# Offsets of rows and weights in SBUF, and the order of the three products of a float32 matrix product

## The reference

```
x = x + conv(x, W0) + cond @ cw0.T + bias
x = x + agg_w1 @ x + agg_b1        # agg_w = sum_k att[b, k] * weight[k]
x = x + agg_w2 @ x + agg_b2
x = x + conv(x, W1) + cond @ cw1.T + bias
```

## Time and profile before

| | us |
|---|---|
| median of 3 runs | 2548.53 (2548.13 to 2550.66) |
| the profiled execution | 2548.97 |
| its span | 2547.1 |
| TensorE (PE) busy | 2520.7 (99%) |
| ScalarE (ACT) busy | 2252.2 (88%) |
| VectorE (DVE) busy | 1995.5 (78%) |
| mean busy share of DMA, main queue | 87.3% |

### The profile page before, as it was taken

How to read it: one execution, slowest core, us unless ns; L and a number is a source line. 1 busy time by engine, 2 the same in 40 slices (tenths; PEclk the granted TensorE clock), 3 DMA queues, 4 the chain that set the end, 5 groups by cost and what they waited for, 6 DMA issues and landing times.

```text
span 2547.1 us, 43755 instructions
## 1 busy us (share of the span) xinstructions
PE 2520.7 (99%) x11068; PEld 2062.1 (81%) x11068; DVE 1995.5 (78%) x5032; ACT 2252.2 (88%) x2449; POOL 16.0 (1%) x27
## 2 busy tenths in 40 slices
PE   7999999999999999999999999999999999999997
PEld 6888888888888888888888888888888888888886
DVE  8777787778777878787877778777877787888784
ACT  6889998999899989998998899899989998998895
POOL 2000000000000000000000000000000000000000
PEclk9999999999999999999999999999999999999999
DMA  7889889888888888899889888988888888888986
GB/s 257 318 332 331 328 324 334 329 328 325 332 328 327 329 333 326 325 333 328 329 326 333 330 329 324 333 329 329 325 333 329 327 327 333 325 326 333 329 312 235
DMA packets 334986, 825.56 MB, mean 324 GB/s; under 512 B 37370, under 2 KB 39426, under 8 KB 302210
## 3 DMA queue, kind: packets, MB, share of 16 engines
q1 hardware_dynamic: 332736, 823.94, 87.3%
q10 hardware_dynamic: 2242, 1.53, 0.2%
HBM read 137.97 MB, written 134.23 MB: 107 GB/s over the span
## 4 chain that ended last, share of the span: by engine, by line
PE 97%; DVE 1%; DMA 1%; ACT 1%; SPq 0%; issue 0%; ACTq 0%; DVEq 0%
PE pair L930 82%; PE quad L980 14%; PE pair L970 1%; DVE partial L754 0%; DMA x_ch<-x_ph 0%; DMA mix<-att_saved 0%; ACT x_ch L473 0%; ACT x_out L525 0%; DVE operands L790 0%; DMA x_ph<-in_small 0%; DVE operands L787 0%; DMA x_ph<-x_ch 0%; SPq L318 0%; SPq L370 0%; DVE operands L714 0%
## 5 line engine op out<-in xcount | busy, mean ns | idle before, releaser
L930 PE MATMUL pair<-operands 128*128 128x512 f32 x9216 | 2157.3, 393 | 3.4 <-DVE operands L805 1.8
L930 PEld LDWEIGHTS pair<-operands 128*128 128x128 f32 x9216 | 1722.6, 188 | 385.8 <-DVE operands L805 2.2
L473 ACT COPY x_ch<-x_in 128x1088 f32<-128x1088 f32 x255 | 556.9, 2184 | 0.0
L787 DVE CAST operands<-x_ch 128x512 fp32r<-128x512 f32 x512 | 205.4, 422 | 437.4 <-DMA x_ch<-x_ph 437.4
L525 ACT COPY x_out<-x_ch 128x1024 f32<-128x1024 f32 x252 | 524.2, 2080 | 0.2 <-DMA x_ch<-x_ph 0.2
L542 ACT ACTIVATE x_ph<-pair,bias_now 128x512 f32<-128x512 f32 x508 | 354.8, 699 | 187.6 <-PE pair L930 187.6
L533 ACT ACTIVATE x_ph<-pair,bias_now 128x512 f32<-128x512 f32 x512 | 357.5, 698 | 77.5 <-PE pair L930 69.7
L754 DVE SCALAR_TENSOR_TENSOR partial<-expert,mix,partial 128x128 f32<-128x128 f32 x1536 | 416.4, 349 | 0.0
L980 PE MATMUL quad<-operands 128*128 128x512 f32 x1536 | 372.9, 392 | 2.4 <-DVE operands L790 2.4
L805 DVE TENSOR_TENSOR operands<-x_ph,operands 128x542 fp32r<-128x542 f32 x512 | 357.7, 721 | 0.0
L980 PEld LDWEIGHTS quad<-operands 128*128 128x128 f32 x1536 | 289.7, 189 | 66.6 <-issue 3.1
(11 more groups left out here) (77 smaller groups left out, 214.2 us busy)
## 6 DMA issues: line engine op xcount, KB each, us to landing
x_ch<-x_ph SPq DMA_DIRECT2D x1024, 256.0 KB, 3.0
x_ph<-x_ch SPq DMA_DIRECT2D x512, 272.0 KB, 2.9
x_ph<-x_ch SPq DMA_DIRECT2D x512, 271.0 KB, 2.6
x_in<-in_x SPq DMA_DIRECT2D x128, 1024.0 KB, 5.7
out<-x_out SPq DMA_DIRECT2D x128, 1024.0 KB, 4.3
x_out<-in_W SPq DMA_DIRECT2D x8, 144.0 KB, 4.4
expert<-in_e ACTq DMA_DIRECT2D x2, 512.0 KB, 8.5
mix<-att_saved SPq DMA_DIRECT2D x2, 512.0 KB, 6.8
```

The lines of the kernel that those rows point to most:

```text
L473: nc.scalar.copy(to, of).then_inc(x_cut, 1)
L930: mm = nc.tensor.matmul(conv_bank[g % 2], w[l][:, m, g, :], x[:, g, m * SEG:m * SEG + N], start=(m == 0 and x is hi and w is w_hi), stop=( ...
```

## The change

Three things change. The tile `operands` is laid out anew: rows of x and x3 stand 560 elements apart in place of 544, weights of group and group 432 in place of 416, the low rows start 16 elements (modulo 64) before the high rows, the high weights 16 before the low ones, and x1 and the middle matrix start at 48 modulo 64. The three products are issued in the order high weights x low rows, high weights x high rows, low weights x high rows, in the convolutions and in the middle, and the first of them opens the bank. The tile grows by 560 elements, and the two tiles att_t move into a part of x3_ch that is free during the start.

```diff
--- before.py
+++ after.py
@@ -42,6 +42,7 @@
     RUN = N // SEG
     EDGE = HALO * SEG
     ROW = N + 2 * EDGE
+    PITCH = ROW + SEG
     MARGIN = HALO * PH
     K = a["e0"].shape[0]
     DMA = 16
@@ -68,29 +69,36 @@
 
 
         NEXT_BLOCK = C + SEG
-        NEXT_GROUP = BLK * C + ROW - N
-        WEIGHTS = G * BLK * C + C
-        operands = sb("operands", [C, 4 * G * ROW + 2 * L + 4 * WEIGHTS + 2 * C], f32r)
-        ends = [0]
-
-        def operand(width):
-
-            ends.append(ends[-1] + width)
-            return operands[:, ends[-2]:ends[-1]]
-
-        x_hi, x_lo, x3_hi, x3_lo = (
-            operand(G * ROW).rearrange("c (g n) -> c g n", g=G)
-            for _ in range(4))
-        x1_hi, x1_lo = (operand(L).rearrange("c (p n) -> c p n", p=PH) for _ in range(2))
-
-
-        def in_phase(columns):
-
-            return bass.AP(tensor=columns.tensor, offset=columns.offset,
-                           ap=[columns.ap[0], [NEXT_BLOCK, BLK], [NEXT_GROUP, G], [1, C]])
-
-        w_hi, w_lo = ([in_phase(operand(WEIGHTS)) for l in range(2)] for _ in range(2))
-        m_hi, m_lo = (operand(C) for _ in range(2))
+        NEXT_GROUP = BLK * NEXT_BLOCK
+        WEIGHTS = (G * BLK - 1) * NEXT_BLOCK + C
+        TURN = 4 * SEG
+        ROWS = 2 * G * PITCH
+        LAYER = -(-2 * WEIGHTS // TURN) * TURN
+        LAST = 3 * SEG
+        operands = sb("operands", [C, 2 * ROWS + 2 * LAYER + LAST + 2 * L + 2 * C], f32r)
+
+        def operand(first, width):
+
+            return operands[:, first:first + width]
+
+        def rows_at(first):
+
+            return operand(first, G * PITCH).rearrange("c (g n) -> c g n", g=G)[:, :, 0:ROW]
+
+        def weights_at(first):
+
+            at = operand(first, WEIGHTS)
+            return bass.AP(tensor=at.tensor, offset=at.offset,
+                           ap=[at.ap[0], [NEXT_BLOCK, BLK], [NEXT_GROUP, G], [1, C]])
+
+        (x_hi, x_lo), (x3_hi, x3_lo) = ((rows_at(l * ROWS), rows_at(l * ROWS + ROWS // 2 - SEG))
+                                        for l in range(2))
+        w_lo = [weights_at(2 * ROWS + l * LAYER) for l in range(2)]
+        w_hi = [weights_at(2 * ROWS + l * LAYER + WEIGHTS) for l in range(2)]
+        MIDDLE = 2 * ROWS + 2 * LAYER + LAST
+        x1_hi, x1_lo = (operand(MIDDLE + n * L, L).rearrange("c (p n) -> c p n", p=PH)
+                        for n in range(2))
+        m_hi, m_lo = (operand(MIDDLE + 2 * L + n * C, C) for n in range(2))
 
         x_in = sb("x_in", [C, ODD, L + 2 * MARGIN])
         x_ch = sb("x_ch", [C, PH, ROW])
@@ -139,7 +147,6 @@
         total = [sb(f"total{l}", [B, 1]) for l in range(2)]
         share = [sb(f"share{l}", [B, 1]) for l in range(2)]
         att = [sb(f"att{l}", [B, K]) for l in range(2)]
-        att_t = [sb(f"att_t{l}", [K, B]) for l in range(2)]
 
         vec_part = x3_ch[:, :, :].rearrange("p q n -> p (q n)")[:, 0:B * K].rearrange(
             "p (b k) -> p b k", k=K)
@@ -157,6 +164,7 @@
         w0, w1, cw, w2, b0, b1 = ([take(width) for l in range(2)] for width in (C, C, C, K, 1, 1))
         spare = x3_ch[:, PH // 2:, :].rearrange("p q n -> p (q n)")
         h1, h2 = ([spare[:, (2 * n + l) * B:(2 * n + l + 1) * B] for l in range(2)] for n in range(2))
+        att_t = [spare[0:K, (4 + l) * B:(5 + l) * B] for l in range(2)]
         spread_g = x4_ph[:, 0, 0:G * C].rearrange("p (g c) -> p g c", g=G)
 
         pair = [ctx.enter_context(nc.psum_tensor(f"pair{n}", [C, 2, N], f32)) for n in range(2)]
@@ -926,9 +934,9 @@
 
             def conv(l, g, hi, lo, done):
                 for m in range(BLK):
-                    for w, x in ((w_hi, hi), (w_hi, lo), (w_lo, hi)):
+                    for w, x in ((w_hi, lo), (w_hi, hi), (w_lo, hi)):
                         mm = nc.tensor.matmul(conv_bank[g % 2], w[l][:, m, g, :], x[:, g, m * SEG:m * SEG + N],
-                                              start=(m == 0 and x is hi and w is w_hi),
+                                              start=(m == 0 and x is lo),
                                               stop=(m == BLK - 1 and w is w_lo))
                 mm.then_inc(done, 1)
 
@@ -976,9 +984,9 @@
                 pe.wait_ge(m_split, 2 * b + 2)
                 for q in range(PH):
                     pe.wait_ge(x1_split, PH * b + q + 1)
-                    for m, x in ((m_hi, x1_hi), (m_hi, x1_lo), (m_lo, x1_hi)):
+                    for m, x in ((m_hi, x1_lo), (m_hi, x1_hi), (m_lo, x1_hi)):
                         mm = nc.tensor.matmul(mid_bank[:, q, :], m[:, :], x[:, q, :],
-                                              start=(m is m_hi and x is x1_hi), stop=(m is m_lo))
+                                              start=(x is x1_lo), stop=(m is m_lo))
                     mm.then_inc(mid_done, 1)
 
             def step(b):
```

## The result

The changed kernel takes 2560.03 us (median of 5 runs, 2559.3 to 2562.54) against 2548.53 us before (also 5 runs): the ratio is 1.0045, with a 95% interval from 1.0032 to 1.0058. It is slower by 11.5 us; 2522 us had been forecast.

What follows compares the result with a forecast made beforehand. PE, busy 99%, was taken to bound the kernel through its product spacing: 2549.0 - 33 (spacing) + 2.5 (re-entry) + 1.3 (a) + 2.5 (b) = 2522.3, forecast 2522 us. The 8-in-10 range was 2512 to 2551 us.

Steps and rivals of the forecast that it cites:

- The spacing: Convolution products on PE would go from 230.2 to 226.7 ns apart: 0.26 us a batch, 33 us over 126 turns.
- Rival 1: Row-offset jumps between products cost, not rows-to-load distance; three a group instead of two, 16 us slower, 2565 us; chance 0.09.
- Rival 2: Offsets do nothing, something else separates convolution and middle products; 2549 us, within 0.2%; chance 0.12.
- Rival 3: Products get faster, but gapped rows of x_hi and x_lo cost DVE 0.46 us in L714; 2541 us; chance 0.07.
- Rival 4: Sharing at every product brings the spacing to about 220 ns, until waits bind; 2482 us; chance 0.03.
- The re-entry: After L970's passes or a late load, PE's products need to settle: 20 ns a batch, 2.5 us added.
- (a): Convolution 4's first group waits for ACT's third x1 evacuation to empty its bank: 0.01 us a batch, 1.3 us added.
- the 0.11 us of leeway: How late a PE load may be without a stall, read from load spacing at L970; the value taken for (a).
- the 0.04: How late a PE load may be by the record: 0.227 us a product less 0.188 a load.
- (b): conv1 of the next batch waits for low rows from L714 on DVE, mean slack 0.26 us: 2.5 us added.
- The sum: Profiled 2549.0 us less 33 plus 2.5, 1.3 and 2.5 gives 2522.3; forecast 2522, own range 2513 to 2536.

Runs made afterwards that it cites:

- everything shared and two steps: Kernel before with weights read from windows so every load lies at the rows' offset, rows still making 2 steps a group (wrong weights): 2551.6 us.
- the kernel without steps: Kernel before with rows pitch 576, weights 128 apart, every block reading block 0's rows, so all start at 0 modulo 64 elements (wrong rows): 2531.28 us.
- the constant distance: The kernel without steps with all weights moved 16 elements (modulo 64) away from the rows throughout: 2587.3 us.

## Why the prediction was wrong

**The spacing.** The step that failed is "I take 226.7 ns for every product of the stream, the value of the only stretch of the trace where all pairs share their offset". That row does not show what was read from it. The middle has two properties at once: shared offsets, and no change of offset at all. The prediction read the first as the cause. The kernel with everything shared and two steps has the first and not the second, and runs at the pace of before; the kernel without steps has both and runs at 226.7 ns once settled. In place of 226.7 ns the changed kernel shows 231.5 ns. What the convolutions pay for is the steps, 36 cycles or 15 ns each in the kernel before, in the changed one and in the one with everything shared, and the changed kernel bought the sharing with a third step in every group: the low rows 16 below the high ones. Over the eight groups of a turn the excess rose by 30, 8, 36, 30, 20, 26, 47 and 36 cycles, 97 ns together; 6 ns came back where the middle is entered; a turn became 91 ns longer.

**Rival 1** said this, with 15.75 ns a step (31.5 ns for two) and 2565 us at a chance of 0.09. Its price was right to 5%; it came out 5 us too high, because it charged the third step in full in all 8 groups, and in those behind L970 and the conv4 wait a disturbance that is there anyway covers part of it (8 cycles more in the second group, 20 and 26 in the fifth and sixth). It was not right in all: it ruled out a price for the distance, which the constant distance shows, and of its signs three raised products a group did not come, all nine are raised. Its weight was the mistake. The argument against it was that "a jump is only another start address"; the trace held a hint the other way: the product beside the first load apart is among the fastest of its group (542), and the ones after it are slow (548 550 560), which fits a step better than a distance. It is a hint alone, since the second load apart stands beside a slow product (560). The prediction used means of 70 products, where this does not show.

**Rival 2** (offsets do nothing) is refuted by 2531 and 2587 us for the same work at other offsets. Where the weights lie does bear on the pace: moving them alone by 64 bytes took the products from 544 cycles to 554 and 566 in turn, 6.7 ns more in the mean. By what way is not shown.

**Rival 3**, the forms: 2422 ns against 2419, nothing. **Rival 4**: no product pair was seen to settle below 544 cycles.

**The re-entry** was put at 20 ns a batch, from the two slow products that open the middle. Those are the tail of the last group's step: in the kernel without steps they are gone. That kernel has the re-entry alone, 79 + 49 cycles, 53 ns, 7 us in all and not 2.5.

**The waits.** (a) In the changed kernel the third evacuation ends at 1208.28 and the load follows 0.06 us later, 0.00 us behind its product: the slower PE has relaxed it (in the mean that load starts 3 ns behind the product before it, and 18 ns in the kernel before). In the kernel without steps it starts 70 ns behind, and the next product is hardly late (551 cycles, 7 over 544), so the 0.11 us of leeway read from L970 was nearer than the 0.04. (b) was taken too low: 0.05 us a batch in the kernel without steps, 6 us in all, against 2.5 taken and 4 to 8 worked out for the turns read. Had the pace come as forecast, the time would have been about 2531 us, as in that kernel: inside the range, and 9 us above the forecast.

**The sum.** The range of the sum itself, 2513 to 2536, does not follow from its own bounds, which give 2516 to 2539 us. That changes nothing in the outcome.

**Still open:** what a step does inside TensorE or SBUF, whether the rows' step or the loads' is what costs, why a lone +16 step whose load runs one product ahead costs 84 cycles or more where two of them a group cost 72, and why nine steps in quick turn cost 92 and not 324.

## What to carry to other kernels

When a stretch of a trace is fast, list everything in which it differs from the slow one before naming one as the cause, and look at single distances in order, not at means: which product is slow, the one with the suspected fault or the one behind it. Where products follow each other without a gap, keep the start offset of rows and weights the same, modulo 256 bytes, from one product to the next: here 2531.3 us without steps against 2548.5 with two a group. A layout that only makes them change together gained nothing: 2551.6 us. And before paying for a faster PE, find the slack of the chain beside it: here it was 0.26 us a batch in the mean but 0.11 and 0.41 in turn, and of the 0.20 us that PE won without steps, 0.05 were lost to it.

## What the runs showed of the hardware

At a granted clock of 1.00, products of 512 columns with fp32r operands never settled below 544 cycles from start to start, 226.7 ns. At 0.50 eight of the middle stood 427 ns apart; half of that, 213.3 ns, is the 512 cycles of the scale used here, 32 fewer than 544. With the weights' load 16 elements beyond the rows the distance is 560 in the mean (554 and 566 in turn), with the rows 32 beyond the weights 560 (550 and 570), with the rows 16 beyond only 549 (542, 550, 556): the distance has a sign. A step of +16 that rows and load make together, twice a group, raises three products by 12, 14 and 10 cycles. Some jumps cost nothing, all of them by whole multiples of 64 elements: in the kernel without steps the rows go 2304 elements on from high to low and 576 on from group to group, the weights 128 on from block to block, and the products stay at 544. One of 32 does cost (24 cycles for +32, rows and weights together). After the two short passes of L970 the products are disturbed even where rows and weights share one offset: 88 cycles (37 ns) over eight distances and 10 more in the next group, in the turns of the kernel without steps in which PE did not wait. With the constant distance nothing is added to its 16 cycles a product there: 128 over the same eight.
